# Layer norm, feed-forward block and circulant filter on one core: the first weight piece on ScalarE's DMA queue, and its low part made between the two normalised halves of chunk 0

## The reference

```python
xn = layernorm(x)                         # over the 256 columns, eps 1e-5
D = fractal_dimension(xn)                 # from the first 1024 numbers of xn
x1 = ifft(fft(xn) * wave_filter(D)).real  # a circulant filter on the columns
bits = sigmoid(x1 @ W_el + b_el) > 0.5    # 24 bits a row
attn = x1 + golay_correct(bits) @ W_le + b_le
ffn = gelu(xn @ w1 + b1) @ w2 + b2        # 256 -> 1024 -> 256
out = x + attn + ffn
```

## Time and profile before

| | |
|---|---|
| median of 3 runs | 415.88 us (415.7 to 415.95) |
| profiled execution | 415.92 us |
| its span in the trace | 414.1 us |
| granted TensorE clock | 0.998 |
| TensorE busy | 406.1 us |
| VectorE busy | 307.2 us |
| ScalarE busy | 218.7 us |
| GpSimd busy | 73.8 us |

### The profile page before, as it was taken

One profiled execution on the slowest core, in us unless ns is written; L12 is line 12 of the kernel. 1 busy time (PEld: TensorE's weight loads), 2 busy tenths in 40 slices (PEclk: granted clock), 3 DMA queues, 4 the chain that ended last, 5 costly groups with the idle time before them and its releaser, 6 DMA issues.

```text
span 414.1 us, 5561 instructions
## 1 busy us (share of the span) xinstructions
PE 406.1 (98%) x1785; PEld 325.0 (78%) x1785; DVE 307.2 (74%) x503; ACT 218.7 (53%) x325; POOL 73.8 (18%) x102
## 2 busy tenths in 40 slices
PE   8998999999999999999999999999999999999996
PEld 4786788887878888788888878888788887878874
DVE  7889696868679676786868678686786868676654
ACT  3957436555364554536554464554536655464641
POOL 2162321212012121111212012121111212012000
PEclk9999999999999999999999999999999999999999
DMA  7562323123332123332122333123333111111011
GB/s 217 182 205 102 102 72 109 49 77 102 101 102 71 51 81 101 102 101 80 54 70 102 101 102 97 24 82 101 102 101 99 53 51 51 51 51 52 0 51 51
DMA packets 16495, 35.78 MB, mean 86 GB/s; under 512 B 5452, under 2 KB 8164, under 8 KB 16484
## 3 DMA queue, kind: packets, MB, share of 16 engines
q1 hardware_dynamic: 16340, 35.52, 27.4%
q10 hardware_dynamic: 144, 0.13, 0.1%
HBM read 27.19 MB, written 8.45 MB: 86 GB/s over the span
## 4 chain that ended last, share of the span: by engine, by line
PE 93%; DVE 4%; DMA 1%; issue 1%; ACT 0%; POOL 0%; SPq 0%; DVEq 0%
PE p_h L884 41%; PE p_f L902 27%; PE p_f L907 14%; PE p_s L939 5%; PE p_l L928 3%; PE p_s L958 2%; PE p_g L952 1%; DMA x_sb<-x 1%; DVE stats L569 1%; DVE xt_sb L644 0%; DVE xt_sb L650 0%; DVE xT_lo L601 0%; DVE w_lo L732 0%; DVE h_lo L611 0%; DVE xt_sb L726 0%
## 5 line engine op out<-in xcount | busy, mean ns | idle before, releaser
L433 ACT ACTIVATE h<-p_h,small_sb 128x512 f32<-128x512 f32 x128 | 88.2, 689 | 152.8 <-PE p_h L884 150.0
L611 DVE TENSOR_TENSOR h_lo<-h,h_hi 128x512 fp32r<-128x512 f32 x128 | 90.0, 704 | 69.6 <-ACT h_hi L441 69.5
L902 PE MATMUL p_f<-h_hi,w_hi 128*128 128x512 f32 x254 | 99.5, 392 | 0.0
L902 PE MATMUL p_f<-h_hi,w_lo 128*128 128x512 f32 x254 | 98.9, 389 | 0.0
L884 PE MATMUL p_h<-xT_hi,w_hi 128*128 128x512 f32 (+1 forms) x258 | 85.6, 413 | 1.5 <-DVE xT_lo L601 1.0
L441 ACT CAST h_hi<-h 128x512 fp32r<-128x512 f32 x128 | 79.4, 620 | 5.8
L884 PE MATMUL p_h<-xT_hi,w_lo 128*128 128x512 f32 (+1 forms) x258 | 79.3, 389 | 0.0
L884 PE MATMUL p_h<-xT_lo,w_hi 128*128 128x512 f32 (+1 forms) x258 | 79.2, 388 | 0.1
L907 PE MATMUL p_f<-h_lo,w_hi 128*128 128x512 f32 x254 | 78.2, 389 | 0.0
L363 POOL TENSOR_TENSOR uv<-xn 128x512 f32<-128x512 f32 x30 | 43.6, 1472 | 126.3 <-DVE xn L596 126.3
L884 PEld LDWEIGHTS p_h<-xT_hi,w_hi 128*128 128x128 f32 x258 | 48.3, 189 | 11.7 <-DVE xT_lo L601 1.5
(11 more groups left out here) (114 smaller groups left out, 328.4 us busy)
## 6 DMA issues: line engine op xcount, KB each, us to landing
xt_sb<-xt SPq DMA_DIRECT2D x16, 512.0 KB, 5.3
x_sb<-x SPq DMA_DIRECT2D x15, 512.0 KB, 4.6
rows_sb<-rows_dram SPq DMA_DIRECT2D x15, 512.0 KB, 4.4
out<-xt_sb SPq DMA_DIRECT2D x15, 512.0 KB, 2.9
xt_sb<-w SPq DMA_DIRECT2D x3, 512.0 KB, 8.3
xt_sb<-w SPq DMA_DIRECT2D x2, 256.0 KB, 4.1
x_sb<-x SPq DMA_DIRECT2D x2, 128.0 KB, 2.3
x_sb<-x SPq DMA_DIRECT2D x1, 256.0 KB, 3.0
```

Source lines behind the costliest of these rows:

```text
L433: nc.scalar.activation(h[m % 2][:], p_h[:, m % 2, :], ACT.Gelu, bias=small_sb[:, S_B1 + m:S_B1 + m + 1]).then_inc(gelu_done, 1)
L611: nc.vector.tensor_tensor(h_lo[m % HR][:], h[m % 2][:], h_hi[m % HR][:].bitcast(F32), ALU.subtract).then_inc(h_lo_done, 1)
L902: mm(p_f[:, a, :], w[:, m, a * HF:(a + 1) * HF], h_hi[r][:], start=(m == 0 and w is w2_hi), stop=False, skip_group_check=True)
```

## The change

SP no longer issues the load of w1's first piece. ScalarE issues it as its first instruction, ahead of its wait for GpSimd's constants. And VectorE runs `w1_part_lo(0)` between `normalise(0)` and `normalise(1)` instead of behind both.

```diff
             sp.dma_start(id_sb[:], ident).then_inc(id_in, 16)
-            load_w1(0)
             sp.dma_start(small_sb[:], small).then_inc(small_in, 16)
             load_w1(1)
...
         @block.scalar
         def _(act):
 
+            first = slice(0, W1_LOADS[0][1] * P)
+            act.dma_start(w1_f[:, :, first], w1[:, first].rearrange("(k p) h -> p k h", p=P)).then_inc(w1_in[0], 16)
             act.wait_ge(pool_set, 2)
             nc.scalar.activation(early[:], eps[:], ACT.Gelu)
...
             aggregate(0, range(HALF, CT))
-            for g in range(2):
-                normalise(g)
+            normalise(0)
             w1_part_lo(0)
+            normalise(1)
             for g in range(2):
                 dve.wait_ge(t0_hi, g + 1)
```

## The result

The changed kernel takes 417.74 us (median of 8 runs, 417.23 to 419.75) against 415.93 before (8 runs, 415.70 to 416.18). The ratio is 1.005, 95% interval 1.0037 to 1.0063: slower, by 1.8 us in the median, where 0.75 was forecast. The profiled execution is the fastest of the eight, 417.23 us with a span of 415.4, so it shows 1.31 us of loss and not the typical 1.8. Its granted clock is 0.994, and in all eight runs it was 0.992 to 0.995; for the kernel before the profiled run has 0.998, and of its 83 runs beside the experiments 82 have 0.997 or more.

The account below looks back on a forecast made before the run. TensorE's stream was taken to bound the kernel, any delay at chunk 0's start reaching the end. x's delay + 0.80, VectorE's move + 0.05 and the clock - 0.10 gave + 0.75 us, median 416.6, range 415.9 to 417.3.

Parts of the forecast that it names:

- What bounds the kernel: Whole kernel: TensorE carries 93% of the chain that ended last, so a change elsewhere matters only where TensorE waits.
- a delay of chunk 0's stream is carried to the end: Start of chunk 0: whatever moves TensorE's stream at 9 to 11 us reaches the end one for one.
- The delay of x behind the weights: Loads at the start: x yields DMA engines to the weights, third piece + 0.80 us, landing at 5.44; chance 0.66.
- two queues that alternate: DMA engines at the start: weights through together with x's second piece, x's third piece behind all of them.
- in time: GpSimd's root of the first half: ready by 6.3 at most, before the first normalising at 6.42.
- the upper bound, 1.26: x's landing: 1.26 us late if no idle DMA share is filled and the weights go at 208 GB/s.
- the lower bound of 0.73: x's landing: 0.73 us late if all the DMA engines' idle share up to 4.05 could be filled.
- The gain is 0 to 0.05 us: Moving `w_lo` on VectorE: frees only the first half's low part; the second half's path passes `w_lo` by.
- a cost of 0 to 0.08: VectorE: `w_lo` between the halves makes the second normalising late by 0 to 0.08 us; 0.05 taken.
- One thing comes back: TensorE's transposes: starting at 8.56, behind the clock's rise, they run at the high level and save 0.10 us.
- Rival C: TensorE at chunk 0: x late leaves idle gaps, the clock rises later, 417.8 with half the matmuls hit; chance 0.14.
- Against it: Argument on the clock rival: a gap of 1.04 us before 34.09 leaves no low-level stretch behind it.

Follow-up runs that it names:

- filled load-only kernel: Changed kernel with VectorE's old order, so only the load on ScalarE's queue, plus five extra idle matmuls in TensorE's gaps: median 416.61 us, ratio 1.0014.
- two filled kernels: Five extra idle matmuls added to the changed kernel (median 417.16 us), and to the changed kernel with VectorE's old order (median 416.61 us).
- load-only kernel: Changed kernel with VectorE's old order, so only the weights' load on ScalarE's queue differs from the kernel before: median 416.73 us, ratio 1.0028.
- the move alone: Kernel before with only VectorE's new order, `w_lo` between the two normalisings, weights still on SP's queue: median 417.67 us, ratio 1.0037.
- the small load: Changed kernel loading only 16 of 256 columns of the first weight piece, the rest set to a constant by GpSimd: median 417.31 us, ratio 1.0029.
- the two inputs: Kernel before with an extra VectorE subtraction of `w_lo`'s size, two SBUF inputs, between the two normalisings: median 416.51 us, ratio 1.0016.
- filled changed kernel: Changed kernel with five more idle matmuls, three behind the first aggregate of chunk 0's statistics and two behind the second: median 417.16 us, ratio 1.0032.

## Why the prediction was wrong, point by point

- **What bounds the kernel, and that a delay of chunk 0's stream is carried to the end:** right. Low product 9.77 to 11.21, sum into `p_g` + 1.35, chunk 1's first matmul 34.09 to 35.43, the end + 1.31.
- **The delay of x behind the weights:** right in mechanism and near in size. I took + 0.80 for the third piece, and its statistics start 0.74 later (5.40 against 4.66); the filled load-only kernel measures + 0.62 in time. The landings came in the order that the prediction drew from two queues that alternate (the weights ahead of ScalarE's cast at 4.26, x's second piece at 4.58, the third behind both), but the third wasn't charged with all of the 1.05 to 1.26. One part of the way was other than I wrote: the second piece was later still (its statistics 1.08 later), the first half's root ended at 6.46 and not "in time", and the second piece heads the chain. That the second normalising came at 7.75 (forecast 7.77) and the transposes at 8.53 (8.56) is partly luck. The second root was ready at 7.49 and not at 7.68, and `w_lo` filled the difference. With 512 KB the third piece's statistics start 2.53 later than before (7.19 against 4.66). That is the upper bound, 1.26, for twice the bytes, while 256 KB came out at the lower bound of 0.73; why the two fall on different bounds isn't shown.
- **"The gain is 0 to 0.05 us", "a cost of 0 to 0.08" for the move on VectorE:** the first holds, as even with nearly no bytes to load nothing was gained. The second is the first failed step, and it failed in two ways. It took the hole of 0.59 over from the old profile, when the load shrinks it to 0.32; in the traced run without a held-up root `w_lo` cost 0.22. And it priced `w_lo` only by VectorE's own time and took the root's length as given. But the root runs on GpSimd at that very moment, and `w_lo` reads two tiles of SBUF. Where it is listed 0.11 behind the root, the root lasts 1.35 instead of 0.70 to 0.76 and the second half is 0.6 late. I had looked at what is queued behind `w_lo` on its engine, and not at what runs beside it on the next.
- **"One thing comes back", - 0.10 from the clock:** the second failed step, with its sign wrong. I read the step of 0.20 from 8.12 to 8.32 as the low level and so placed the rise behind it. But the two filled kernels, whose extra idle matmuls ahead ran at the high level (512 columns in 0.22), have the same step of 0.19 to 0.20 behind their transposes and the same 0.66 for these. So the kernel before had its rise ahead of the transposes of 7.71, at most just behind its idle matmuls, and there was nothing to save: from these transposes to the second half's low product it takes 2.06, like both filled kernels (8.19 to 10.25 and 8.40 to 10.46). In the changed kernel the clock rose during the idle matmuls, TensorE idled 2.10, and it was at 0.50 from 8 to 10 us; the transposes took 1.11, and that way 2.68, so + 0.6 stood in place of the - 0.10, of which some 0.5 was left at the sum into `p_g`.
- **Rival C, 0.14:** this is what decided, together with the held-up root, and its chance was far too low: 13 of 14 runs of the changed kernel had a fallen clock, against 1 of 83 of the kernel before. Its mechanism was also told too narrowly, as a first rise that comes late, when the profile shows a fall after the rise; its 417.8 happens to be near the median. "Against it" I had set the gap of 1.04 at 34 us. That gap is half as long and has 25 us of nearly unbroken work ahead of it; it said little on a gap of 2 us behind idle matmuls. The kernel with 8 idle matmuls shows that the gap suffices, in 3 of its 8 runs by the mean clock.
- **How the 1.8 us divide:** x's delay 0.62; `w_lo` in a hole too small for it 0.22, or the held-up root 0.6 where it happens; the clock the rest. Two runs are traced. One (+ 1.31) has x's delay, the 0.22 and the fallen clock, the other (+ 1.34) x's delay and the held-up root with a clock of 0.998. In how many of the changed kernel's runs the root is held up, and whether runs of 419 have both, stays open, as does why the changed kernel's clock falls so much more often than the load-only kernel's (13 of 14 against 4 of 11). A second gap, between the halves' transposes, may be the reason. It is 1.14 to 1.21 in the traces of the move alone, the small load and the two inputs, whose clocks fell in 4 of 7, 5 of 10 and 2 of 12 runs though x was hardly late, and the changed kernel can have it on top of the first. But none of the traces with such a gap shows a fall, and the changed kernel's fall is traced without it, so no run tells this apart. The scatter of the filled changed kernel (417.0 to 418.5 in four runs) isn't explained either. With VectorE's old order the same filling left 0.5 us of scatter, so it comes with the move; a held-up root may be in it, but would give 0.4 more than the 0.2 that the trace has, and not 1.8.

## What to carry to other kernels

A hole in one engine's timeline is only free if it is still there under the change (here it shrank from 0.59 to 0.32) and if the neighbour that sits beside it is asked too: while GpSimd works on the path, put an operation with one SBUF input there, not a subtraction of two SBUF tiles. A transfer issued at once on a second queue isn't early for nothing: it takes the engines from the transfers that head the chain, and a transfer moved off the first queue can as well come much later. And where idle matmuls hold TensorE's clock until the first real work, whatever delays that work has two prices, its own and the clock's, so price the gap from several runs and not from one profile.

## What was not expected of the hardware

- A root of 128x2 elements on GpSimd lasted 1.35 us instead of 0.70 to 0.76 beside a two-input subtraction of 0.68 us that was listed 0.11 behind it (in the traces of four kernels), 0.75 beside a normalising with one SBUF tile as input, and 0.70 where the subtraction came 0.33 to 0.35 behind it.
- The weights' load on ScalarE's queue, issued 0.37 us later than it had been on SP's, was usable 2.6 us later (8.79 against 6.16).
- ScalarE's DMA issue went out at 0.90 though an activation that ends at 2.2 stands ahead of it; only a wait on a semaphore held it.
- The same 12 idle matmuls took from 4.09 to 5.30 us in the profiles: the first rise of the clock comes at another moment of the program from run to run, and the granted clock in the records reads 1.00 before it.
